# Three-pass hot keys and values, a gate bias added on VectorE, and one stage list per engine

## What is computed

```python
# block 0, for each batch
mem = ctx @ W_mem.T                                   # 512 x 256
attn = softmax(x @ mem.T / sqrt(256))
c = attn @ mem
gate = sigmoid(concat(x, c) @ W_gate.T + b_gate)
x = rmsnorm(x + gate * c) * norm_w
# block 1
q = layernorm(x) @ Wq / 8                             # 16 heads of 64
k, v = split(ctx @ Wkv)
sim = where(mask, q @ k.T, lowest)                    # mask: True beyond the valid context
x = x + tanh(attn_gate) * (softmax(sim) @ v) @ Wo
x = x + tanh(ff_gate) * gelu(layernorm(x) @ W1) @ W2
```

## Time and profile before

| | |
|---|---|
| median of 3 runs | 214.29 us (214.09 to 511.52) |
| the profiled execution | 214.26 us |
| its span | 212.4 us |
| TensorE busy | 206.2 us, 97% |
| VectorE busy | 149.9 us, 71% |
| ScalarE busy | 128.1 us, 60% |
| GpSimd busy | 71.2 us, 34% |
| chain that ended last | 83% of the span on TensorE |

### The profile page before, as it was taken

How to read it: one execution, slowest core, us unless ns; L and a number is a source line. 1 busy time by engine, 2 the same in 40 slices (tenths; PEclk the granted TensorE clock), 3 DMA queues, 4 the chain that set the end, 5 groups by cost and what they waited for, 6 DMA issues and landing times.

```text
span 212.4 us, 4471 instructions
## 1 busy us (share of the span) xinstructions
PE 206.2 (97%) x1491; PEld 168.6 (79%) x1491; DVE 149.9 (71%) x527; ACT 128.1 (60%) x411; POOL 71.2 (34%) x70
## 2 busy tenths in 40 slices
PE   7999999999999999999999999999989999999993
PEld 3577746998679888888988798888767899988993
DVE  1679888689988858796879679999948764234310
ACT  3368073689964683884694396997598740158300
POOL 2010043373647031526331524968031906000000
PEclk9999999999999999999999999999999999999999
DMA  6994500014000000000000000000600000100011
GB/s 201 332 361 148 197 0 2 3 14 185 3 0 2 3 2 0 5 2 0 3 2 0 3 2 3 0 0 5 197 2 3 0 0 29 51 25 0 11 45 57
DMA packets 8657, 10.06 MB, mean 47 GB/s; under 512 B 1074, under 2 KB 7732, under 8 KB 8372
## 3 DMA queue, kind: packets, MB, share of 16 engines
q1 hardware_dynamic: 7956, 9.32, 13.0%
q10 hardware_dynamic: 672, 0.39, 0.7%
HBM read 8.66 MB, written 1.05 MB: 46 GB/s over the span
## 4 chain that ended last, share of the span: by engine, by line
PE 83%; ACT 5%; DMA 3%; issue 3%; DVE 2%; SPq 1%; DVEq 0%; ACTq 0%
PE bank L435 47%; PE bank L1226 7%; PE bank L1198 7%; PE bank L1327 6%; ACT expd L667 4%; PE bank L1236 3%; DMA ctx_sb<-in_ctx_dram 3%; PE bank L1276 3%; PE bank L1290 3%; PE bank L1181 2%; SPq L473 1%; PE bank L1266 1%; PE bank L1106 1%; DVE oT_pair L991 1%; PE bank L1129 1%
## 5 line engine op out<-in xcount | busy, mean ns | idle before, releaser
L542 POOL TENSOR_TENSOR probs<-expd,row_rcp 128x512 f32<-128x512 f32 x39 | 41.8, 1092 | 64.0 <-DVE row_rcp L901 64.0
L667 ACT ACTIVATE expd<-expd,neg_max 128x128 f32<-128x128 f32 x128 | 49.6, 393 | 1.9 <-DVE neg_max L891 1.8
L891 DVE CUSTOM_DVE_ANT_0 expd<-bank,mask_bias 128x128 f32<-128x128 f32 x128 | 28.6, 285 | 4.3 <-PE bank L1198 2.6
L435 PE MATMUL bank<-wo_pair,oT_pair 128*128 128x256 f32 x192 | 26.8, 290 | 0.2 <-DVE x_sb L1017 0.2
L435 PE MATMUL bank<-xhT_pair,wq_pair 128*128 128x256 f32 x192 | 26.1, 287 | 0.0
L435 PEld LDWEIGHTS bank<-wo_pair,oT_pair 128*128 128x128 f32 x192 | 24.1, 190 | 2.4 <-issue 2.1
L435 PEld LDWEIGHTS bank<-xhT_pair,wq_pair 128*128 128x128 f32 x192 | 23.8, 191 | 1.4 <-DVE xhT_pair L961 0.6
L667 ACT ACTIVATION_READ_ACCUMULATOR expd<-expd,neg_max 128x1 f32 x128 | 24.5, 192 | 0.0
L435 PE MATMUL bank<-wq_pair,gelu_pair 128*128 128x256 f32 x192 | 23.6, 283 | 0.1
L435 PEld LDWEIGHTS bank<-wq_pair,gelu_pair 128*128 128x128 f32 x192 | 23.3, 192 | 0.4 <-DVE x_sb L1059 0.3
L1226 PE MATMUL bank<-ident,probs 128*128 128x128 f32 x160 | 21.4, 276 | 0.0
(11 more groups left out here) (147 smaller groups left out, 349.3 us busy)
## 6 DMA issues: line engine op xcount, KB each, us to landing
stage<-in_L_xattn_W_dram SPq DMA_DIRECT2D x2, 1024.0 KB, 5.0
x_sb<-in_x_dram SPq DMA_DIRECT2D x4, 256.0 KB, 7.5
wkv_sb<-in_L_xattn_Wkv_dram SPq DMA_DIRECT2D x2, 512.0 KB, 5.3
stage<-in_L_xattn_Wq_dram SPq DMA_DIRECT2D x1, 1024.0 KB, 9.1
stage<-in_L_xattn_Wo_dram SPq DMA_DIRECT2D x1, 1024.0 KB, 5.3
out_dram<-x_sb SPq DMA_DIRECT2D x8, 128.0 KB, 1.9
ctx_sb<-in_ctx_dram SPq DMA_DIRECT2D x4, 192.0 KB, 6.1
probs<-in_L_xattn_W_gate_dram SPq DMA_DIRECT2D x1, 512.0 KB, 7.7
```

Of the source, the lines that this page charges most:

```text
L435: last = nc.tensor.matmul(bank_ap, lhs(a), rhs(c), start=start and n == 0, stop=stop and n == 2)
L542: nc.gpsimd.tensor_tensor(probs[:, r, :].rearrange("p (h k) -> p h k", h=hb), expd[:, r, :].rearrange("p (h k) -> p h k", h=hb), row_rcp[: ...
L667: last = nc.scalar.activation(here, here, ACT.Exp, bias=neg_max[:, r, h:h + 1], scale=-1.0, accum_out=row_sum[:, r, h:h + 1])
L891: last = nc.vector.tensor_tensor_reduce(expd[:, r, h * w:(h + 1) * w], SC[n % 2][:, h * w:(h + 1) * w], mask_bias[:, first:first + w], -1. ...
```

## The change

1. The eight key stages, and the value stages of tiles 1 to 3 (six), become `split_matmul`. The two value stages of tile 0 stay fp32.
2. New stages make their parts. hotpair: ScalarE casts the four hot tiles of ctxT (128x512), VectorE subtracts. splitk: ScalarE casts the key weights (128x1024) into `wo_pair`'s high part, VectorE subtracts in place. splitv: ScalarE casts the value weights, GpSimd subtracts in place, after the two fp32 value stages have read them. splito waits until the keys are done, as its buffer holds the key weights.
3. The bias matmul goes, with all that builds its operands. b_gate is loaded to all 128 partitions. VectorE adds it from PSUM into `th`, then ScalarE's tanh works in `th`. VectorE's multiplies follow as before.
4. Four lists take the place of one: `TENSOR_ORDER`, `SCALAR_ORDER`, `VECTOR_ORDER`, `POOL_ORDER`. Banks go by TensorE's list. An assertion keeps the stages of one kind in one order across the lists. The branch stands at another place in each list: TensorE now branches after y(0), before ctxT("hot") and the first scores.

The diff, cut:

```diff
+TENSOR_ORDER = (
+    ("xT", 0), ("ctxT", 0), ("tiles",), ("y", 0), ("look", "PE"), ("branch", "PE"), ("dummy", 0), ("ctxT", "hot"),
+    ("scores", "ctx", 0, 0), ("dummy", 1), ("v", "hot", 0, 0), ("v", "hot", 0, 1), ("weights",),
+    ("spread", "ctx", 0, 0), ("xT", 1), ("ctxT", 1), ("gatemem",), ("u", 0), ("k", "hot", 0), ("k", "hot", 1),
+    ("gate", 0), ("k", "hot", 2), ("k", "hot", 3), ("k", "hot", 4), ("y", 1), ("v", "hot", 1, 0),
+    ("scores", "ctx", 1, 0), ("k", "hot", 5), ("k", "hot", 6), ("v", "hot", 1, 1), ("xhT", 0), ("v", "hot", 2, 0),
+    ("xT", 2), ("k", "hot", 7), ("ctxT", 2), ("spread", "ctx", 1, 0), ("q", 0, 0), ("q", 0, 1), ("ctxT", 3),
+    ("scores", "head", 0, 0), ("u", 1), ("q", 0, 2), ("scores", "head", 0, 1), ("gate", 1),
...
+    ("h2T", 0, 0), ("spread", "head", 2, 3), ("wo", 2, 1), ("scores", "head", 3, 2), ("av", 2, 3),
+    ("spread", "head", 3, 0), ("h2T", 0, 1), ("wo", 2, 2), ("scores", "head", 3, 3), ("av", 3, 0), ("wo", 2, 3),
+    ("spread", "head", 3, 1), ("ff1", 0, 0), ("ff1", 0, 1), ("wo", 3, 0), ("spread", "head", 3, 2), ("av", 3, 1),
...
+SCALAR_ORDER = (
+    ("wmem",), ("xT", 0), ("xpair",), ("y", 0), ("branch", "ACT"), ("hotpair",), ("exp", "ctx", 0, 0),
+    ("v", "hot", 0, 0), ("weights",), ("splitk",), ("spread", "ctx", 0, 0), ("xT", 1), ("splitq", 0), ("gatemem",),
+    ("u", 0), ("splitq", 1), ("k", "hot", 0), ("splitv",), ("gate", 0), ("k", "hot", 1), ("k", "hot", 2),
+    ("fuse", 0), ("k", "hot", 3), ("k", "hot", 4), ("y", 1), ("mask",), ("rms", 0), ("rms", 1), ("rms", 2),
...
+VECTOR_ORDER = (
+    ("wmem",), ("any",), ("xT", 0), ("ctxT", 0), ("flag",), ("branch", "DVE"), ("ctxT", "hot"), ("xpair",),
+    ("scores", "ctx", 0, 0), ("hotpair",), ("norm", "ctx", 0, 0), ("v", "hot", 0, 0), ("v", "hot", 0, 1),
+    ("weights",), ("spread", "ctx", 0, 0), ("splitk",), ("xT", 1), ("ctxT", 1), ("gatemem",), ("u", 0),
+    ("splitq", 0), ("splitq", 1), ("k", "hot", 0), ("k", "hot", 1), ("gate", 0), ("k", "hot", 2), ("k", "hot", 3),
+    ("lnq",), ("rms", 0), ("scores", "ctx", 1, 0), ("xhat", 0), ("k", "hot", 4), ("k", "hot", 5),
...
+POOL_ORDER = (
+    ("norm", "ctx", 0, 0), ("branch", "POOL"), ("splitv",), ("rms", 0), ("norm", "ctx", 1, 0), ("xhat", 0),
+    ("splito", 0), ("splito", 1), ("norm", "head", 0, 0), ("norm", "head", 0, 1), ("rms", 1),
...
-            load(bgate_rows, b_gate.rearrange("(a d) -> a d", a=1).to_broadcast([2, D]), w_in["bgate"])
+            load(bgate_sb[:, :], b_gate.rearrange("(a d) -> a d", a=1).to_broadcast([P, D]), w_in["bgate"])
...
+                    elif st[0] == "splitv":
+                        gp.wait_ge(act["kvhi"], path.kv_no(st))
+                        gp.wait_ge(pe["v"], 2)
+                        nc.gpsimd.tensor_tensor(wkv_lo[:, INNER:2 * INNER], wkv_sb[:, INNER:2 * INNER],
+                                                value_hi[:, :].bitcast(F32), ALU.subtract).then_inc(pool["kvlo"], 1)
...
                     elif kind == "gate":
                         for t in range(T):
-                            sc.wait_ge(pe["gate"], T * (c - 1) + t + 1)
-                            if c > 1:
-                                sc.wait_ge(act["square"], c - 1)
-
-                            nc.scalar.activation(th[:, t, :], path.bank(st, t)[:, 0:D], ACT.Tanh, scale=0.5
+                            sc.wait_ge(dve["gatein"], T * (c - 1) + t + 1)
+                            nc.scalar.activation(th[:, t, :], th[:, t, :], ACT.Tanh, scale=0.5
                                                  ).then_inc(act["tanh"], 1)
...
+                    elif kind == "hotpair":
+                        sc.wait_ge(dve["ctxT"], path.hot_keys_in())
+                        nc.scalar.copy(hot_pair[HI][:, :, :], hot_keys).then_inc(act["hot"], 1)
...
                     elif kind == "splito":
                         sc.wait_ge(w_in["wo"], 16)
+                        if path.nt == 1:
+                            sc.wait_ge(pe["k"], PAIRS)
...
                     elif kind == "gate":
+                        if c == 1:
+                            ve_.wait_ge(w_in["bgate"], 16)
+                        else:
+                            ve_.wait_ge(act["square"], c - 1)
+                        for t in range(T):
+                            ve_.wait_ge(pe["gate"], T * (c - 1) + t + 1)
+                            nc.vector.tensor_tensor(th[:, t, :], path.bank(st, t)[:, 0:D], bgate_sb[:, :], ALU.add
+                                                    ).then_inc(dve["gatein"], 1)
                         for t in range(T):
                             ve_.wait_ge(act["tanh"], T * (c - 1) + t + 1)
...
+                    elif kind == "splitk":
+                        ve_.wait_ge(act["kvhi"], path.kv_no(st))
+                        nc.vector.tensor_tensor(wkv_lo[:, 0:INNER], wkv_sb[:, 0:INNER],
+                                                key_weights(HI, slice(0, INNER)).bitcast(F32), ALU.subtract
+                                                ).then_inc(dve["kvlo"], 1)
...
-                            nc.tensor.matmul(out_b[:, 0:D], ones_r[:, :], bgate_parts[:, :], start=False, stop=False)
...
+                        if b == "hot":
+                            if c == 1:
+                                te.wait_ge(dve["kvlo"], 1)
+                                te.wait_ge(dve["hot"], 1)
+                            free(path, st)
+                            cols = slice(pair * P, (pair + 1) * P)
+                            split_matmul(path.bank(st)[:, :].rearrange("p (s n) -> p s n", s=KT),
+                                         lambda a: key_weights(a, cols), lambda a: hot_pair[a][:, :, :], True, True
+                                         ).then_inc(pe["k"], 1)
+                            continue
```

More of the change, by code:

```diff
@@ new lines @@
+ORDERS = {"PE": TENSOR_ORDER, "ACT": SCALAR_ORDER, "DVE": VECTOR_ORDER, "POOL": POOL_ORDER}
+GENERAL_BEGIN = (
+    ("any",), ("xT", 0), ("ctxT", 0), ("xpair",), ("y", 0), ("ctxT", "hot"), ("flag",), ("tiles",),
+    ("scores", "ctx", 0, 0), ("norm", "ctx", 0, 0), ("exp", "ctx", 0, 0), ("weights",), ("spread", "ctx", 0, 0),
+    ("ctxT", 1), ("xT", 1), ("wmem",), ("gatemem",), ("u", 0), ("splitq", 0), ("splitq", 1), ("gate", 0), ("y", 1),
+    ("rms", 0), ("scores", "ctx", 1, 0), ("fuse", 0), ("xhat", 0), ("norm", "ctx", 1, 0), ("exp", "ctx", 1, 0),
+    ("lnq",), ("ctxT", 2), ("xhT", 0), ("mask",), ("q", 0, 0), ("splito", 0), ("splito", 1), ("ctxT", 3),
@@ L399, in probs_done, with kv_no @@
                 return (dve["probs"], 1) if n == 1 else (pool["probs"], n + 1 - (n > 1))
+            def kv_no(self, st):
+                return 1 + (self.plans["ACT"].index(st) > self.plans["ACT"].index(("splitk",) if st[0] == "splitv" else ("splitv",)))
             def hot_keys_in(self):
@@ L700, in run @@
                         nc.scalar.copy(xhT_pair[:, HI, :, :], q_in[:, :, :]).then_inc(act["xhT"], 1)
+                    elif kind in ("splitk", "splitv"):
+                        half = slice(0, INNER) if kind == "splitk" else slice(INNER, 2 * INNER)
+                        sc.wait_ge(w_in["wkey" if kind == "splitk" else "wvalue"], 16)
+                        nc.scalar.copy(key_weights(HI, half) if kind == "splitk" else value_hi[:, :], wkv_sb[:, half]
+                                       ).then_inc(act["kvhi"], 1)
+                    elif kind == "hotpair":
+                        sc.wait_ge(dve["ctxT"], path.hot_keys_in())
+                        nc.scalar.copy(hot_pair[HI][:, :, :], hot_keys).then_inc(act["hot"], 1)
                     elif kind == "k" and c % 2:
@@ L1280, in run @@
                     elif kind == "v":
                         b, s, h = st[1:]
+                        if b == "hot" and s:
+                            if c == 3:
+                                te.wait_ge(pool["kvlo"], 1)
+                                te.wait_ge(dve["hot"], 1)
+                            free(path, st)
+                            cols = slice(h * BANK, (h + 1) * BANK)
+                            split_matmul(path.bank(st)[:, :], lambda a: hot_pair[a][:, s, :],
+                                         lambda a: value_weights(a, cols), True, True).then_inc(pe["v"], 1)
+                            continue
```

222 lines of the change are left out of this document (114 added, 108 removed), and 23 rows, old and new, of tables (HOT_KEYS, SCALAR_ORDER, TENSOR_ORDER, VECTOR_ORDER).

## The result

The changed kernel takes 211.97 us (median of 6 runs, 211.71 to 212.01), the kernel before beside it 214.24 us: ratio 0.9895, 95% interval 0.988 to 0.991. On a second chip it took 211.86 us, ratio 0.9874. The profiled execution took 211.99 us with a span of 210.2 us. The forecast was 211.6 us. The total is nearly right; what each part of the change is worth by itself is not. One of the six runs of the kernel before took 511.52 us and stands outside the ratio.

The account below looks back on a forecast made before the run. TensorE's own matmuls were taken to bound the kernel; 214.26 - 2.38 (passes) - 0.96 (bias) + 0.38 + 0.1 (start) + 0.9 (early waits) - 0.7 (later waits) = 211.6 us. Forecast 210.0 to 213.2; wider range 208.7 to 214.2.

Parts of the forecast that it names:

- The price on TensorE: Matmul work: each of 14 key and value stages 0.69 us instead of 0.86, bias matmul 0.12 us removed eight times.
- The passes' term, -2.38: Hot key and value stages: 14 fp32 matmuls become three passes each, saving 2.38 us.
- VectorE becomes the bound: Rival, 12.5 to 62 us: VectorE's net 2.3 us go on the path, matmul savings become waits; 216.2 us, chance 0.10.
- The bias was too small, -0.96: Gates: dropping eight bias matmuls of 0.12 us saves 0.96 us; VectorE adds the bias instead.
- The early waits, +0.9: First 40 us: new TensorE waits, chiefly on VectorE around the first gate, cost 0.9 us, bounds 0.3 and 2.0.
- The count of VectorE against TensorE: Start to first gate: following both lists by operation times, VectorE reaches the gate's adds near 22.0 us, level with TensorE.
- the rule: VectorE operations with two SBUF inputs and GpSimd operations reading SBUF exclude each other; up to 2.38 us of VectorE blocked.
- the row: L1003's subtraction beside working GpSimd, 2.07 us against 1.22 at L997; splitv may slow VectorE by up to 0.8 us.
- The later waits, -0.7: 40.5 to 209 us: new lists save half of TensorE's 1.35 us idle, 0.7 us; bounds -1.35 and +1.5.
- The start, +0.48: Before the gate weights: ctxT(1) moved behind them costs 0.38 us, and the weights slip by 0.1 us.
- the three passes are no cheaper: Rival, key and value stages: weight loads show between parts, so only the bias is saved; 214.0 us, chance 0.13.

Follow-up runs that it names:

- the first experiment: Changed kernel with the 14 hot key and value stages as single fp32 matmuls again, without hotpair, splitk, splitv: 211.84 us, ratio 0.9875.
- third question: Stage starts of the changed kernel compared with its fp32 keys and values version; then xhat(1) moved ahead on GpSimd's list: 211.1 us, with fp32 211.77 us.

## Why the total was right and the steps were not

**The price on TensorE held.** Key and value stages take 0.70 us in the trace, the old bias 0.24 us per gate (0.12 for each half), as the earlier trace rows said; busy time fell by 3.1 us where 3.3 was forecast. The Trainium skill (FP8 and Floating Point Precision, TensorE Precision Notes), by which three passes would take 0.65 us (an estimate, 0.75 of the 0.86 us of the fp32 stage), is slightly too low here.

**The passes' term, -2.38, held as work and failed as a gain.** It stood on the sentence that a microsecond of matmul removed is a microsecond gained, unless TensorE then waits. Between 12 and 62 us VectorE was busy 42.9 of 49.5 us already, and 13 of the 14 stages stand there. Undoing the passes gives TensorE 2.24 us more to do and takes away nearly as much waiting; the expectation of the first experiment had 0.6 us of waits go with them. The rival "VectorE becomes the bound" had the right place, and even the right sentence on the savings becoming waits, but as a single outcome with a chance of 0.10 and a price of 216.2. It came true for the passes alone and at no further loss.

**The bias was too small, -0.96.** Under the new lists it is worth 1.6 us with fp32 keys and 2.5 with the passes by the medians, 1.2 and 1.8 by the profiled executions. The matmul is 0.95 of that. With the passes, the three small operations at 18.9 to 20.1 us, ahead of u's low part on VectorE, add 0.64 us of waiting; the prediction took them off VectorE's busy time and not off a chain. With fp32 keys that wait is not there. The rest is in no wait that shows: stage by stage, both kernels with the old bias get 0.4 to 0.5 us back where the kernels with the addition wait (about 25, 48 and 60 us), and lose 0.55 us between 123 and 141 us. Why they lose it there stays open. Under the old list the same edit is worth 0.0. The added operations do lengthen the gate's chain, as forecast, and the query stage at 47.99 us waits 0.25 us for it, but leaving them out altogether bought nothing.

**The early waits, +0.9.** The term was for the first 40 us. TensorE's idle time there is 0.30 + 0.28 = 0.58 us, of which 0.30 is the wait for W_gate's load, so 0.28 us stands against VectorE, where the prediction's lower bound was 0.3. But modelled ends hide part of a wait. By the starts of the stages (third question) the key stages and y(1) at the first gate's banks lose 0.56 us and the query stage behind L1047 0.38, which makes 0.94. So the size held. The first of the two places was named, the second was not, and gatemem and u, which were to wait too, show no wait. The count of VectorE against TensorE was made with each operation at its undisturbed length, and L1047 came out at 1.17 us. The prediction looked for such an effect at splitv only, and took 0.85 us from L1003 in place of the rule. At splitv, one 0.42 us multiply took 0.65, and 1.58 us in the kernel without a bias: there the rule (wait until GpSimd has finished) describes it, and the row did not bound it.

**The later waits, -0.7.** By idle time they did not fall: from 40.5 to 156 us TensorE had no work for 0.16 + 0.02 + 0.98 = 1.16 us before and for 0.56 + 0.00 + 0.75 = 1.31 us now. The hole at 126 to 156 us is 0.23 smaller, and 40.5 to 62 us has 0.40 more, most of it at the query stage behind the second gate and at xhat(1), which lasted 2.17 us behind GpSimd. Yet the new lists alone gained 0.9 us, and not by closing holes: stage by stage from the gate weights on, wo takes 0.84 us less than before, the keys 0.80 and ff1 0.42 less, the head scores 0.77 more. Such differences are too short to show as idle, so the term was sized from the wrong view.

**The start, +0.48.** The bare stretch behind y(0) is there, 0.65 us as a wait, and ctxT(1) moved behind the weights, as forecast (0.38 of the term). The weights begin at 13.11 us, 0.6 later than before, where 0.1 was forecast: W_gate's load landed at 4.75 + 8.31 = 13.06 us by the chain of waits. In a second profile of the same kernel they begin at 12.73. I had cost the transfers at nothing.

In sum, there are two ways to hold the forecast against the runs. Along the path, from the first matmul of the gate weights to the start of the last matmul, the kernel before takes 196.10 us and the changed one 193.60. Work off TensorE is 14 x 0.16 + 0.95 = 3.2 us; ctxT(1) adds 0.38 and the early waits 0.94; so everything later is 0.6 us shorter, where 0.7 was forecast, with 0.8 us lost at 57 us inside it that no term had. Outside that stretch the start cost 0.5 us more than forecast, and the end, from the last matmul on, is 0.27 us shorter. Part by part, by undoing them, the forecast fails: the lists bring 0.9 us where I expected nothing, the bias 1.6 where I expected 0.6, the passes nothing where I expected 1.8. That these errors cancel to 0.4 us in the total is luck. The range from 208.7 to 214.2 held the time because it was built from rivals, one of which ("the three passes are no cheaper", 214.0) describes their lack of effect, though for another reason than the one that came true.

## What to carry to other kernels

Removing work from the busiest engine paid nothing here in a stretch where a second engine was nearly as full: check the windows, not the page's total. When VectorE and GpSimd both work on SBUF, look at which starts first around each operation that TensorE waits for, and order the lists so that the one on the path goes first; moving one entry was worth more here than 14 stages at 20% less. Undo a part both alone and with the others before it gets a price: the passes were worth a loss of 2.2 us, a loss of 0.5 to 0.95, nothing and a gain of 0.7 in four different surroundings.

## What the hardware showed that I had not expected

- VectorE's fp32 operation with a scalar (xhat, 128x256, two of them in 0.73 us alone) was held by two GpSimd operations of which the first had begun 0.06 us earlier, to 2.17 us; 0.1 us the other way round the two took 1.43. GpSimd's own operation is not spared: splitv took 2.54 us in the changed kernel and 3.68 with the bias matmul, where it began 0.93 us after a pair of VectorE subtractions that lasted 2.34 (seen once, not tested).
- Pauses of 0.90 and 0.85 us in two stretches of 3 us, one single pause of 1.24 us among them, were followed by the lower level of the granted clock (mean 0.58 over 27 to 30 us), with score matmuls at 3.35 us in place of 1.94. Pauses of 0.74 and 1.04 us in the stretches from 30 to 36 us of the same kernel, and the bare 0.65 us after the branch of the changed kernel, had no such effect: the clock stayed full.
- Loads issued in the same order landed at different times and moved the start: W_gate's load took 8.3 us in one profile of the changed kernel and 7.4 in another, and the gate weights began at 13.11 and at 12.73 us (211.99 and 211.78 us in all).
